# One expert-routed feed-forward kernel: three late tiles placed by selection instead of four, and the work around the first routing turn and the first expert in another order

## What is computed

```python
h = jnp.einsum('bsd,bdh->bsh', x, W[cat_ids]) + b[cat_ids][:, None, :]
xf = h.reshape(t, d)
probs = jax.nn.softmax(xf @ Wr, axis=-1)
eidx = jnp.argmax(probs, axis=-1)              # expert of each token
rank = ...                                      # place of a token among its expert's
keep = rank < cap                               # cap = 512
xe = xf[dispatch]                               # (8, 512, 512)
hid = jnp.maximum(jnp.einsum('ecd,edf->ecf', xe, W1), 0.0)
ye = jnp.einsum('ecf,efd->ecd', hid, W2)        # scaled by the token's probability
out = x + (ye put back at the tokens' rows)
```

## Time and profile before

| | us |
|---|---|
| median of 3 runs | 797.53 |
| lowest and highest of them | 797.40, 797.59 |
| the profiled execution | 798.6 |
| its span, first to last instruction | 796.8 |

### The profile page before, as it was taken

The page is one execution under the profiler, slowest core; times in us unless marked ns, Lnnn a source line. Parts: engine busy times, 40 slices in busy tenths (PEclk is TensorE's granted clock), DMA queues, the critical chain, the costliest instruction groups (busy, mean ns, idle before and its releaser), DMA issues.

```text
span 796.8 us, 14206 instructions
## 1 busy us (share of the span) xinstructions
PE 789.2 (99%) x5255; PEld 702.3 (88%) x5255; DVE 586.8 (74%) x765; ACT 350.2 (44%) x537; POOL 531.8 (67%) x392
## 2 busy tenths in 40 slices
PE   9999999999999999999999999999999999999997
PEld 6788889899999999999999999999999999999996
DVE  5678978768757895798767876788578866896532
ACT  3322347346444554455444644454445444454430
POOL 1000158857889688887888788778887889754601
PEclk9999999999999999999999999999999999999999
DMA  8988544531544355534434454425542545255201
GB/s 272 367 311 295 212 153 159 185 126 58 190 158 157 106 178 174 162 118 171 164 133 157 150 174 149 156 67 176 177 128 86 186 169 168 105 184 179 71 1 54
DMA packets 61103, 127.20 MB, mean 160 GB/s; under 512 B 8310, under 2 KB 8310, under 8 KB 60562
## 3 DMA queue, kind: packets, MB, share of 16 engines
q1 hardware_dynamic: 47714, 95.19, 34.3%
q0 software_dynamic: 13216, 31.38, 12.0%
q10 hardware_dynamic: 144, 0.26, 0.1%
HBM read 110.13 MB, written 25.17 MB: 170 GB/s over the span
## 4 chain that ended last, share of the span: by engine, by line
PE 95%; DMA 1%; DVE 1%; SPq 1%; issue 0%; ACT 0%; POOL 0%; POOLq 0%
PE y_ps L1512 44%; PE acc_ps L1410 20%; PE tp_ps L1410 19%; PE acc_ps L1329 6%; PE tp_ps L1329 3%; DMA x_more<-x_t 1%; PE tp_ps L1258 1%; PE acc_ps L1424 1%; PE tp_ps L1424 1%; PE y_ps L1243 0%; DVE xt_split L846 0%; DVE late_rest L953 0%; DVE late_parts L959 0%; PE y_ps L1279 0%; SPq L389 0%
## 5 line engine op out<-in xcount | busy, mean ns | idle before, releaser
L1512 PE MATMUL y_ps<-w_split,xt_split 128*128 128x512 f32 x1536 | 365.6, 391 | 0.0
L1512 PEld LDWEIGHTS y_ps<-w_split,xt_split 128*128 128x128 f32 x1536 | 282.6, 188 | 54.8
L1410 PE MATMUL acc_ps<-x_split,w_split 128*128 128x256 f32 x1320 | 181.0, 283 | 0.0
L1410 PE MATMUL tp_ps<-x_split,w_split 128*128 128x256 f32 x1284 | 176.5, 283 | 0.0
L1410 PEld LDWEIGHTS acc_ps<-x_split,w_split 128*128 128x128 f32 x1320 | 171.1, 192 | 3.7 <-DVE tp_ps L1066 0.2
L1410 PEld LDWEIGHTS tp_ps<-x_split,w_split 128*128 128x128 f32 x1284 | 166.8, 192 | 3.8 <-ACT logits_t L739 0.2
L554 POOL DMA_INDIRECT rows<-h_rows,idx_all x112 | 137.6, 1229 | 33.0 <-issue 32.4
L976 DVE TENSOR_TENSOR w_split<-stage,w_split 128x1024 fp32r<-128x1024 f32 x64 | 101.1, 1610 | 44.4 <-ACT w_split L680 44.4
L965 DVE TENSOR_TENSOR w_split<-w_sums,w_split 128x1024 fp32r<-128x1024 f32 x62 | 96.3, 1555 | 2.8 <-ACT w_split L673 2.8
L673 ACT ACTIVATE w_split<-stage 128x1024 fp32r<-128x1024 f32 x64 | 53.9, 842 | 90.4 <-PE tp_ps L1410 43.0
L742 ACT ACTIVATE xt_split<-tp_ps 128x512 fp32r<-128x512 f32 x64 | 38.2, 597 | 122.0 <-PE tp_ps L1410 119.3
(11 more groups left out here) (183 smaller groups left out, 819.0 us busy)
## 6 DMA issues: line engine op xcount, KB each, us to landing
stage<-w SPq DMA_DIRECT2D x64, 1024.0 KB, 7.4
b_rows<-x SPq DMA_DIRECT2D x8, 1024.0 KB, 9.6
h_rows<-rows POOLq DMA_DIRECT2D x6, 1024.0 KB, 9.2
stage<-cond_wt SPq DMA_DIRECT2D x4, 1024.0 KB
x_more<-x_t SPq DMA_DIRECT2D x4, 1024.0 KB, 9.9
stage<-x_t SPq DMA_DIRECT2D x3, 1024.0 KB, 8.6
stage<-cond_w SPq DMA_DIRECT2D x3, 1024.0 KB, 9.5
h_rows<-rows SPq DMA_DIRECT2D x8, 256.0 KB, 2.3
```

Source lines behind the costliest of these rows:

```text
L1410: last = nc.tensor.matmul(out, w1s[wg][:, w, wb, k, f], xes[xg][:, a, xb, k, :], start=start and k == 0 and (w, a) == (HI, HI), stop=True, ...
L1512: last = nc.tensor.matmul(y_ps[:, s, :], hts[:, (q % 2) * QF + jj, a, s * P:(s + 1) * P], w2s[:, q % 2, w, jj, :], start=(first and jj == ...
```

## The change

There are five edits.

1. **Routing weight, bias columns and the first m.** SP loads the routing weight ahead of the bias rows and the conditional matrix, and the four loads of bias columns behind the second conditional matrix. The 32 small matmuls on the bias columns move from `m_turn(0)` to the head of `route(0)`; their result is copied by ACT in `copy_logits(0)`, no longer by DVE in `copy_m(0)`. `SPLIT_W[1]` is (5, 5, 6, 6), no longer (4, 4, 5, 5), and `SPLIT_X[3]` is (7, 9), no longer (6, 7).
2. **`LATE` is 3.** Tile 28 goes through DRAM and the early gathers, which now wait for its store too; 12 selection matmuls fall away.
3. **The last tile in halves.** Its bias add and all its parts are made in two halves of 256 columns.
4. **PE's order of placing** is early 0, early 1, late 0, late 1, early 2, late 2, early 3.
5. **W1.** All four parts of `sum_w1(1)` run on POOL ahead of the store of chunk 5. DVE's remainder of group 0 of W1 moves from tile 23 to tile 29.

```diff
-    SPLIT_X = [None, None, (3, 4), (6, 7), (12, 14), (16, 17), (21, 21), (23, 25)]
-    SPLIT_W = [None, (4, 4, 5, 5), (11, 11, 12, 13), (16, 17, 18, 19)]
+    SPLIT_X = [None, None, (3, 4), (7, 9), (12, 14), (16, 17), (21, 21), (23, 25)]
+    SPLIT_W = [None, (5, 5, 6, 6), (11, 11, 12, 13), (16, 17, 18, 19)]
-    LATE = 4
+    LATE = 3
     SPLIT_W1 = {NT - 9: 0, NT - 6: 3}
+    LOW_W1 = {NT - 6: 3, NT - 3: 0}
...
             load_xt(1)
+            sp.wait_ge(s_wr0, 1)
+            sp.dma_start(wr32[:, :, 0:E], w_r.rearrange("(p k) e -> p k e", p=P)).then_inc(s_wr, 16)
             load_bias_rows(0)
             load_cond_wt(0)
             cats += [load_cat(b) for b in range(1, BATCH)]
-            sp.wait_ge(s_wr0, 1)
-            sp.dma_start(wr32[:, :, 0:E], w_r.rearrange("(p k) e -> p k e", p=P)).then_inc(s_const, 16)
-            for b in range(BATCH):
-                sp.dma_start(b_col[:, b, :], cond_b[bass.ds(cats[b], 1), :].rearrange("o (p k) -> p (o k)", p=P)
-                             ).then_inc(s_const, 16)
...
             load_xt(2)
             sp.wait_ge(s_wlo, DK)
             sp.dma_start(stage[:, 1, :, :], cond_view(1)).then_inc(s_stage[1], 16)
+            for b in range(BATCH):
+                sp.dma_start(b_col[:, b, :], cond_b[bass.ds(cats[b], 1), :].rearrange("o (p k) -> p (o k)", p=P)
+                             ).then_inc(s_bcol, 16)
             load_xt(3)
...
             for c in range(NCH - 2):
+                if c == NCH - 3:
+                    pool.wait_ge(s_acc, NT - 2 * TPC - TPC)
+                    sum_w1(1)
                 store_chunk(c)
...
             gather_early()
-            first_sums(1)
-            pool.wait_ge(s_part[2], LATE)
-            second_sums(1)
             pool.wait_ge(s_hlast, 16 * LATE)
...
             def copy_logits(b):
                 act.wait_ge(s_mcopy, b + 1)
                 act.wait_ge(s_lt, CPB * (b + 1))
-                if b >= 1:
+                if b == 0:
+                    nc.scalar.activation(bias_g[:, :], bias_ps, ACTF.Copy).then_inc(s_bias, 1)
+                    act.wait_ge(s_bias, 1)
+                else:
                     act.wait_ge(s_lgt, b)
...
-            for i in range(LATE):
+            for i in range(LATE - 1):
                 late_first(i)
                 late_second(i)
+            for half in range(2):
+                late_first(LATE - 1, half)
+            for half in range(2):
+                late_second(LATE - 1, half)
...
+                if n == NT - 1:
+                    for half, done in enumerate((s_half, s_accf)):
+                        cols = late_cols(half)
+                        nc.vector.tensor_tensor(rows[:, c % 2, t, cols], cond_bank(n)[:, cols],
+                                                b_rows[:, c // CPB, cols], ALU.add).then_inc(done, 1)
+                    return
...
-                if n >= NT - LATE:
+                if NT - LATE <= n < NT - 1:
                     late_remainder(n - (NT - LATE))
                 if n == NT - 1:
-                    late_third(LATE - 1)
+                    for half in range(2):
+                        late_remainder(LATE - 1, half)
+                    for half in range(2):
+                        late_third(LATE - 1, half)
...
             def route(b):
                 pe.wait_ge(s_mcopy, b + 1)
-                if b >= 1:
+                if b == 0:
+                    pe.wait_ge(s_bcol, 16 * BATCH)
+                    for k in range(DK):
+                        for g in range(NQ):
+                            nc.tensor.matmul(bias_ps[g * G:(g + 1) * G, :], wr32[:, k, :], b_col[:, :, k],
+                                             start=(k == 0), stop=(k == DK - 1))
+                else:
                     pe.wait_ge(s_ltc, b)
...
-            for s in range(SB - 1):
-                add_early(s)
+            add_early(0, range(DK))
+            add_early(1, range(DK))
             add_late(0, range(DK))
-            add_early(SB - 1)
             add_late(1, range(DK))
-            for ks in (range(2), range(2, DK)):
-                add_late(2, ks)
-                add_late(LATE - 1, ks, last=True)
+            add_early(2, range(DK))
+            add_late(LATE - 1, range(DK))
+            add_early(SB - 1, range(DK), last=True)
```

More of the change, by code:

```diff
@@ L327, in first_x, with late_cols, late_count @@
             return first_b12[:, part, :, :] if block == B12 else xes[block[0]][:, part, block[1], :, :]
+        def late_cols(half):
+            return slice(0, D) if half is None else slice(half * D // 2, (half + 1) * D // 2)
+        def late_count(i, half):
+            return i + 1 if half is None else i + 1 + half
         def steps(i, u, per):
@@ L949, in choose_late, with late_remainder, late_third @@
                 last.then_inc(s_late, 1)
[L951 to L960 removed]
+            def late_remainder(i, half=None):
+                dve.wait_ge(s_part[0], late_count(i, half))
+                cols = late_cols(half)
+                nc.vector.tensor_tensor(late_rest[:, i, cols], rows[:, 1, TPC - LATE + i, cols],
+                                        late_parts[:, 0, i, cols], ALU.subtract).then_inc(s_rest, 1)
+            def late_third(i, half=None):
+                dve.wait_ge(s_part[1], late_count(i, half))
+                dve.wait_ge(s_rest, late_count(i, half))
+                cols = late_cols(half)
+                nc.vector.tensor_tensor(late_parts[:, 2, i, cols], late_rest[:, i, cols],
+                                        late_parts[:, 1, i, cols], ALU.subtract).then_inc(s_part[2], 1)
             def split_w1(i, u, grp):
@@ L1235, in m_turn @@
                     pe.wait_ge(s_mcopy, b)
-                if b == 0:
-                    for k in range(DK):
-                        for g in range(NQ):
-                            nc.tensor.matmul(bias_ps[g * G:(g + 1) * G, :], wr32[:, k, :], b_col[:, :, k],
-                                             start=(k == 0), stop=(k == DK - 1))
                 for k in range(DK):
@@ L1370, in by_block, with add_late, add_early @@
                 return rows_of_tile.rearrange("p (r b) -> p b r", b=DK)[:, k, :]
-            def add_late(i, ks, last=False):
+            def add_late(i, ks):
                 for part in range(3):
-                    pe.wait_ge(s_part[part], i + 1)
+                    pe.wait_ge(s_part[part], late_count(i, 1 if i == LATE - 1 else None))
                 for k in ks:
                     for part in range(3):
-                        done = nc.tensor.matmul(y_ps[:, k, bass.ds(at[i], P)], by_block(late_parts[:, part, i, :], k),
-                                                late_sel[:, i, :], start=False, stop=(last and part == 2),
+                        nc.tensor.matmul(y_ps[:, k, bass.ds(at[i], P)], by_block(late_parts[:, part, i, :], k),
+                                                late_sel[:, i, :], start=False, stop=False,
                                                 skip_group_check=True)
+            def add_early(s, ks, last=False):
+                pe.wait_ge(s_hg[s], 16)
+                for k in ks:
+                    done = nc.tensor.matmul(y_ps[:, k, s * P:(s + 1) * P], by_block(early_rows[:, s, :], k), ident[:, :],
+                                            start=(s == 0), stop=last, is_transpose=True, skip_group_check=True)
                     if last:
                         done.then_inc(s_tp, 1)
-            def add_early(s):
-                pe.wait_ge(s_hg[s], 16)
-                for k in range(DK):
-                    nc.tensor.matmul(y_ps[:, k, s * P:(s + 1) * P], by_block(early_rows[:, s, :], k), ident[:, :],
-                                     start=(s == 0), stop=False, is_transpose=True, skip_group_check=True)
             pe.wait_ge(s_late, 1)
             pe.wait_ge(s_tok, 1)
-            for s in range(SB - 1):
-                add_early(s)
+            add_early(0, range(DK))
+            add_early(1, range(DK))
             add_late(0, range(DK))
-            add_early(SB - 1)
             add_late(1, range(DK))
-            for ks in (range(2), range(2, DK)):
-                add_late(2, ks)
-                add_late(LATE - 1, ks, last=True)
+            add_early(2, range(DK))
+            add_late(LATE - 1, range(DK))
+            add_early(SB - 1, range(DK), last=True)
             spread_all()
```

44 lines of the change are left out of this document (18 added, 26 removed).

## The result

| us | before | after |
|---|---|---|
| median (executions) | 797.59 (19) | 799.58 (19) |
| lowest | 796.81 | 798.56 |
| the profiled execution | 798.6 | 799.58 |
| its span | 796.8 | 797.9 |

The medians are 1.99 us apart; the ratio of the interleaved executions is 1.0029, 95% interval 1.0022 to 1.0035. The kernel became slower, by more than the 0.2% that can be told. 799.58 lies outside the range of 796.9 to 799.2 and next to the rival "Slower: the gathers" (799.7).

What follows compares the result with a forecast made beforehand. Matmuls on PE were taken as the bound, filling 789.2 of 796.8 us. First turn -0.45, last turn +0.85 and hand-over with backlog +0.25 gave +0.65: median 798.2, range 796.9 to 799.2.

Steps and rivals of the forecast that it cites:

- Slower: the gathers: Rival at PE's early blocks: gathers land at the slowest seen, 4.5, and the rank stalls 1.6; +2.15, 799.7; chance 0.07.
- First turn, what goes: At the first route, PE's 0.58 wait for DVE's transpose of m disappears; gain called 0.6.
- the 1.07: Median of the runs, 797.53, lies this far below the profiled execution's 798.6; carried over unchanged to the forecast.
- First turn, what comes: New wait of 0.15 at tile 8 for DVE's last remainder of the conditional matrix, bounds 0 and 0.5.
- That rival: Bias columns land late, at 30.1, so PE waits at `route(0)`; +3.0 in all, 800.5; chance 0.06.
- The last turn: W1's sums on POOL hold up DVE's `choose(3)`; PE stalls 0.85 at `rank_of(3)`, bounds 0 and 1.6.
- the rival that they slip through: Small DVE instructions in the last routing turn aren't held up by POOL's sums; -0.3, 797.2; chance 0.27.
- The play hardly depends on the start: Reason for taking 0.85 at the last rank: the DVE and POOL hand-over sequence barely changes with the sums' start.
- the backlog reaches tile 28 as 0.1: DVE, 3.5 late after the last choice of experts, catches up until 0.1 remains at tile 28.
- The hand-over: Before expert 0, the second gather's landing replaces the last part as PE's wait; +0.15, with backlog +0.25.
- land 3.9 after their start: Early gathers, started 3.7 later, keep their profiled landing time; 4.5 each at the slowest.
- the two slower rivals: Bias columns landing late at `route(0)`, 800.5, chance 0.06; gathers landing late at the early blocks, 799.7, chance 0.07.

Runs made afterwards that it cites:

- e1: Kernel before with the first edit alone (routing weight, bias columns and m in the new order); median 797.74 against 797.62, ratio 1.0005.
- e2: Kernel before with the fifth edit alone (all four W1 sums early, group 0's remainder at tile 29); median 797.95, ratio 1.0005.
- e10: e9 with ACT copying the slots ahead of group 3 of W1, whose remainder is made at tile 28 too; median 797.15, ratio 0.9995.
- e7: Changed kernel with the DRAM stores of tiles 29 to 31 held until the four early gathers have landed; median 797.92, ratio 1.0005.
- e9: e7 with DVE's remainder of group 0 of W1 moved from tile 29 to tile 28; median 797.62, ratio 0.9999.
- e8: e4 with W1's sums behind the last rank, group 0's remainder at tile 23 and late blocks in before's order; median 797.99, ratio 1.0011.
- e11: e8 with PE's four register loads of the windows one tile later; median 797.61, ratio 1.0006.
- e6: Changed kernel, unchanged, profiled a second time; one execution of 799.51, span 797.8.
- e4: Changed kernel with four late tiles again and PE placing early 0 to 2, late 0, early 3, late 1 to 3; median 798.37, ratio 1.0010.

## Why the prediction was wrong

**Sum of the shown terms.** Behind the first turn, both profiles of before agree, so the terms can be read off the first table: 0.15 (0.08 in tile 8 and 0.07 at the rank), 0.02, 0.35 (slots), 0.06 and 1.4 (hand-over), together +2.0, less what the first turn gives, 0 to 0.5. Measured: +1.99, by the interval of the ratio 1.75 to 2.8. So the account closes with a first turn that gives nothing or little. The forecast was +0.65 for a measured +1.99, and the miss would have been larger if its stall at the rank, +0.85 where 0.07 came, hadn't stood against its hand-over: two errors of opposite sign.

**First turn, what goes: -0.6.** The mechanism was there: the wait for m is gone, and against the profile used the stretch became 0.84 shorter (0.3 of it is the wait ahead of `m_turn`, which the prediction left as it was). What failed is the sentence "the median of the runs, 797.53, lies 1.07 below the latter, and I carry the difference over to it unchanged". The profiled execution was longer than the median partly because it had that wait for m. So the wait was taken off twice: once as a gain, once with the 1.07. After's profiled execution and its median are equal, 799.58. Without that gain the forecast would have been 798.8, still 0.8 too low. That the new order of the loads might cost time at the start of the kernel was no term at all; e1 leaves it open.

**First turn, what comes: +0.15 at tile 8.** It came as 0.08. DVE's last remainder ended at 32.0, not near 32.4, and PE started tile 8 at 32.18 with no wait in the list; but tile 8 took 2.89 to the next step in after and e1, and 2.81 in before. The bias columns were no matter, as forecast: landed 6.8 to 9.4 after their issues, ahead of `route`, in after and in e1. That rival is out.

**The last turn: +0.85.** The lock was right and the price wrong. Small instructions are held, 1.36, 1.22 and 0.97 instead of about 0.2, so the rival that they slip through has fallen. In after PE stands 0.92 earlier from tile 9 up to there, so the forecast of 92.1 for the end of `prior` reads 91.18 on its clock; it was 90.60. Most of that 0.6 is this: the load landed 0.3 sooner (8.7 after the issue, not 9.0), the first sum started closer behind it, and the four took 5.49 (84.36 to 89.85), not 5.7, since DVE's short instructions slipped in at the joints and held no sum up. The signal was mis-sized too: PE starts 0.06 after `prior` (90.60 to 90.66), not 0.24. So PE had 2.8 of slack from `prior` to its rank (88.65 to 91.51, less 0.06), and a `choose(3)` that ended 2.87 later left a stall of 0.07, which e2 shows alone; the forecast had 3.45 later on a slack of 2.6, and so 0.85. "The play hardly depends on the start" was the false step: behind the slack each tenth of the start counts in full, in a stall that is the small difference of two large numbers. The Trainium skill (SBUF — State Buffer, Who interferes with whom) has the second of the two to issue fully blocked; the trace agrees for 64 columns as well.

**The slots: a step that was missing.** "the backlog reaches tile 28 as 0.1" looked at DVE's end alone. ACT's split of W1 waits for DVE to come by, and ACT's next instruction is the copy of the slots, for which PE waits. That is the 0.35 of after; e10 takes it back by turning the two about.

**The hand-over: +0.25, in fact +1.4 to 1.5.** This is the term that made the kernel slower, and the step that failed. The steps of the gathers but one, the end of the late parts and the 12 matmuls all held; the prediction named the right thing to be late (a gather's landing, not the last part). The start of the gathers held only by the clock: measured from tile 31 (108.94 before, 108.52 after) tile 28's add and with it the gathers are 0.3 later than forecast, where the backlog of DVE was put at 0.1. What was mis-sized is "land 3.9 after their start", with 4.5 for the slowest. The 3.9 is the median of gathers at 103.73 to 107.78. There they had stores beside them as well, those of tiles 28 to 30, and the 4.5 was the sign of it; tile 31's, issued at 113, came behind them all. Moved by 3.7 us, the last two run beside tile 31's store and the second beside tile 30's: 4.7, 5.4 and 5.2. Not the second but the third gather is then the last that PE waits for, at 115.87 instead of 114.1, and PE waits twice. e7 shows the cause by holding the stores: landings of 3.5 to 3.8, and the 1.5 is back. The rest, 0.4 in the second gather's issue, came from the 1024-column remainder that edit 5 had moved beside it (e9).

The rival "Slower: the gathers" had the place and the time (799.7), but for two wrong amounts: a stall of 1.6 at the rank that was 0.1, and landings of 4.5. It got 0.07 because the slowest landing of one profile was taken as the bound. Even at the old place it is none: the fourth gather of e1 landed 5.1 after its start, and those of e8 and e11 up to 5.7. There most of it is hidden, since with four late tiles the gathers start 3 to 4 us sooner, measured from tile 31; three late tiles have no such slack.

**What stays open.** Which of the three stores costs how much wasn't separated; that it is tile 31's above all is read from the times alone. Nor is it shown that gathers are slower in the new place than in the old one: the two profiles of after have 4.6 to 5.4, but e8 and e11 have as much in the old one. And e1's 0.5 by profiles is not in its median; whether the edit gives a few tenths, or loses them again at the start, couldn't be told.

A slip of the sums besides: the two slower rivals have 0.06 and 0.07, together 0.13 and not 0.12.

## What to carry to other kernels

When a transfer is moved in time, its duration doesn't move with it: read from the table of stretches what the DMA engines do at the new place, and take the landing from transfers beside such traffic, out of more than one profile: the longest landing of a single profile is no upper bound. When a wait is present in the profiled execution, ask whether it is in the median too before both the wait and the distance of profile and median are taken off; a second profile of the same kernel tells. A late engine delays not only who reads its result but also whatever the other engines have queued behind their wait for it, and small copies for the bounding engine belong ahead of such a wait.

## What the runs showed of the hardware

- An indirect gather of 128 rows of 2 KB lands 3.3 to 3.8 us after its start with no store beside it (e7, e9, e10). With stores of 256 KB beside it, it takes 4.6 to 5.4 in after and e6 and 3.8 to 5.7 over all other profiles, the first gather aside. The stores, 2.0 alone, take 3.8 and 4.9 beside gathers in after.
- VectorE's instruction of 64 columns with two SBUF inputs is held for the length of a GpSimd sum of 1.3 us: 0.23 became 1.36.
- A VectorE subtraction of 1024 columns with two SBUF inputs lengthens the issue of a GpSimd gather from 1.04 to 1.42 (after and e7 against e9), and in e2 and e4 the third gather's from 1.00 to 1.28. Beside shorter instructions of VectorE it took 1.22 and 1.23 in e8 and e11. The Trainium skill (SBUF — State Buffer, Who interferes with whom) infers that `tensor_tensor` leaves GpSimd's writing of descriptors alone. The issue as a whole isn't left alone here; whether it is the writing of the descriptors or the reading of the row numbers in `tok_all` isn't separated.
- With four register loads on PE's queue, the tile behind them starts 2.9 to 3.2 us after their value is there (e8, e2, e4), and the tile work loses about 0.5 us in e2 and e4 and 1.2 in e8. Put a tile later (e11) the loads cost nothing, and with three of them, in after, no gap shows.
- The start of the program varies between executions: tile 4 began at 16.8 to 17.6 us in the four profiles with the old order of the first loads, and at 17.2 to 18.2 in the nine with the new one.
